# Graph network of four layers on one core: a 256-column scratch fill behind every gather, and fetch places as 16-bit floats

## The reference

```
h = relu(layernorm(x));  x += clip(h + segment_sum(h[src] * edge_weight * w, dst) + 0.1 * h, 0, 1)
h = relu(layernorm(x));  x += h + silu(bilinear(h, segment_sum(silu(bilinear(h[dst], edge_attr_8)) @ W, src))) @ W'
h = relu(layernorm(x));  x += segment_sum((h[src] @ W_rel[edge_type]) * e, dst)       # 90 relations
h = relu(layernorm(x));  w = MLP(edge_attr_6) -> (E, 16, 16)
for i in range(4):       h = gelu(mean over dst of (h[src] @ w) + h @ root_W[i] + root_b[i])
x += h
```

## Time and profile before

| what | value |
|---|---|
| median of 3 runs | 28610.86 us (28602.41 to 28721.83) |
| the profiled execution's own time | 28730.07 us |
| its span, first to last instruction | 28728.3 us |
| PE matmul busy | 22502.9 us (78%) |
| POOL busy | 21497.8 us (75%) |
| DVE busy | 17590.5 us (61%) |
| ACT busy | 14192.2 us (49%) |
| mean granted TensorE clock | 0.864 of full speed |
| HBM traffic | 109 GB/s over the span |

### The profile page before, as it was taken

The page is one execution under the profiler, slowest core; times in us unless marked ns, Lnnn a source line. Parts: engine busy times, 40 slices in busy tenths (PEclk is TensorE's granted clock), DMA queues, the critical chain, the costliest instruction groups (busy, mean ns, idle before and its releaser), DMA issues. The chain is left out here.

```text
span 28728.3 us, 413713 instructions
## 1 busy us (share of the span) xinstructions
PE 22502.9 (78%) x109882; PEld 12362.4 (43%) x109882; DVE 17590.5 (61%) x29340; ACT 14192.2 (49%) x24676; POOL 21497.8 (75%) x31473
## 2 busy tenths in 40 slices
PE   7888668888878888867777777688886888778886
PEld 3444345555545555533434344333333333333333
DVE  5555468888867667744444444566665666656665
ACT  6666511111135444533333333477775777667775
POOL 7888878888867667766667677677777777777777
PEclk9999879999988888877778787799898889888898
DMA  3211235555532222222222222455554555555554
GB/s 98 45 45 44 46 74 92 94 92 94 92 68 66 64 64 65 66 62 87 90 88 94 87 91 92 125 173 173 174 172 142 172 172 174 158 156 171 172 172 138
DMA packets 2201230, 3120.14 MB, mean 109 GB/s; under 512 B 782486, under 2 KB 1548644, under 8 KB 2199460
## 3 DMA queue, kind: packets, MB, share of 16 engines
q1 hardware_dynamic: 1340898, 2927.73, 31.3%
q0 software_dynamic: 790944, 162.36, 8.3%
q10 hardware_dynamic: 69282, 28.92, 0.4%
HBM read 2443.85 MB, written 673.47 MB: 109 GB/s over the span
## 5 line engine op out<-in xcount | busy, mean ns | idle before, releaser
L772 POOL DMA_INDIRECT got<-table,idx x14310 | 14075.9, 984 | 6055.7 <-issue 3081.4
L790 PE MATMUL in_place<-place_hot,tparts 128*128 128x512 fp8e4 (+1 forms) x49950 | 12106.4, 399 | 2647.8 <-ACT place_hot L995 1563.8
L995 ACT ACTIVATE place_hot<-place_b,far_lanes 128x512 fp8e4<-128x512 f32 (+1 forms) x17550 | 10586.2, 683 | 8.8 <-PE in_place L790 8.8
L790 PEld LDWEIGHTS in_place<-place_hot,tparts 128*128 128x128 bf16 x49950 | 5100.3, 105 | 9003.7 <-issue 4843.7
L1599 POOL DMA_INDIRECT added<-rows,add_idx x2160 | 3602.4, 1668 | 714.3 <-issue 654.5
L968 ACT ACTIVATE mask<-contw 128x208 f32 (+2 forms) x1350 | 555.9, 412 | 5970.6 <-DVE run L1129 2705.2
L775 POOL MEMSET rest<- 128x128 f32 (+2 forms) x14310 | 3199.8, 224 | 10.2
L1216 DVE TENSOR_TENSOR prod<-wcopy,got 128x1024 f32<-128x1024 f32 x810 | 991.5, 1227 | 2990.9 <-ACT wcopy L947 1895.6
L1642 PE MATMUL acc<-hot,spread 128*128 128x392 bf16 x12960 | 2545.4, 350 | 0.0
L1107 DVE SCALAR_TENSOR_TENSOR picked<-range_b,range_col,in_place 128x512 f32<-128x512 f16 (+1 forms) x1350 | 962.7, 713 | 2553.8 <-DMA added<-rows,add_idx 2404.6
L1171 DVE TENSOR_TENSOR prod<-w_in,rows_p 128x2048 f32<-128x2048 f32 x810 | 1846.8, 2280 | 444.7 <-ACT rows_p L983 283.7
(11 more groups left out here) (250 smaller groups left out, 21896.4 us busy)
## 6 DMA issues: line engine op xcount, KB each, us to landing
w_in<-kept SPq DMA_DIRECT2D x2430, 512.0 KB
kept<-wcopy SPq DMA_DIRECT2D x810, 512.0 KB
place_b<-place_row SPq DMA_DIRECT2D x1080, 256.0 KB
got<-table,idx POOLq DMA_INDIRECT x14310
attr<-in_edge_attr SPq DMA_DIRECT2D x270, 768.0 KB
range_b<-range_row SPq DMA_DIRECT2D x1080, 128.0 KB
rows<-in_src_row SPq DMA_DIRECT2D x270, 512.0 KB
sums<-outb SPq DMA_DIRECT2D x1350, 96.0 KB
```

The lines of the kernel that those rows point to most:

```text
L772: pool.indirect_dma_start(out=got[:, r, j * W:(j + 1) * W], out_offset=None, in_=table, in_offset=bass.IndirectOffsetOnAxis(ap=idx[:, r, j ...
L790: mm = pe.matmul(in_place[b][:, h, :], tparts[:, s, t, :], place_hot[:, b, t, h * XC:(h + 1) * XC], start=(t == 0 and s == 0), stop=(t == ...
L995: ins = act.activation(place_hot[:, b, t, :], place_b[:, b, :], ACT.Abs_reciprocal_sqrt, bias=SB["far_lanes"][:, t:t + 1], scale=HOT_SLOPE ...
```

## The change

All gathering passes get a fill of 256 columns. The weighted pass has that width already; relational and kernel_kept had 128, kernel_net 32. The row of places is stored and loaded as 16-bit floats. The shift of 2^-12, which a 16-bit place of up to 1,567 could not carry, moves into the bias column `far_lanes`, so that the same argument comes out. Places are whole numbers below 2,048 and stand exactly in 16 bits. No instruction is added, taken away or moved on any engine: one DVE instruction of the preparation (an addition over 3,240 columns) becomes a copy with a cast.

```
+RW = 256
...
-        place_row = dram("place_row", (EP + 2 * CE,))
+        place_row = dram("place_row", (EP + 2 * CE,), F16)
...
-        range16 = sb("range16", [P, T], F16)
+        range16, place16 = sb("range16", [P, T], F16), sb("place16", [P, T], F16)
...
-                for row, v in ((SB["place_row"], key), (SB["range_row"], range16)):
+                for row, v in ((SB["place_row"], place16), (SB["range_row"], range16)):
...
-                c.step(dve.tensor_scalar(key[:, :], key[:, :], PLACE_SHIFT, None, ALU.add))
+                c.step(dve.tensor_copy(place16[:, :], key[:, :]))
...
-        rest = sb("rest", [P, {"weighted": 256, "relational": 128, "kernel_net": 32, "kernel_kept": 128}[kind] * J0])
+        rest = sb("rest", [P, J0 * RW])
         src_at = sb("src_at", [P, T], I32)
-        RW = rest.shape[1] // J0
...
-            place_b = sb("place_b", [P, HALVES, XE])
+            place_b = sb("place_b", [P, HALVES, XE], F16)
...
-        "const_far_lanes": -lanes() * np.float32(HOT_SLOPE),
+        "const_far_lanes": (PLACE_SHIFT - lanes()) * np.float32(HOT_SLOPE),
```

## The result

The changed kernel takes 27848.6 us (median of 4 runs, 27823.51 to 27856.5) where the kernel before takes 28660.6 beside it: a ratio of 0.9715 [0.9688, 0.9742]. It is 2.8% **faster**. The profiled execution took 27823.5 us, with a span of 27821.7.

A forecast was written before the change was run, and what follows sets the result against it. POOL bounds the weighted pass, the ACT, PE and DVE ring the kept ones; elsewhere POOL's idle time covers wider fills. Terms 0 + 0 + 20 + 90 = +110 us on 28611 gave 28720 us, 0.4% longer; forecast 28640 to 28800, range 28560 to 28950.

The forecast's parts named there:

- What bounds the kernel now: All passes: POOL limits the weighted pass; elsewhere it waits for indices, 310 to 1011 us a pass, cover for wider fills.
- Covered three times over: 0: Relational pass: wider fills add 260 us of POOL, hidden by 816 us of its idle time, so 0.
- single waits of 29 us: kernel_net: POOL's single index waits reach 29 us, read as users going very unevenly, so the ring can run dry.
- I take 20, close to the low end: kernel_net: fills add 635 us of POOL against 930 us of cover; +20 us from a range of 0 to 635.
- I take 90, near the middle: Three kept passes: 253 us more POOL each overruns the cover; +90 us, between 62 and 132 in all.
- The floor: Kept passes: POOL's wider fills overrun its cover by 28, 16 and 18 us, so POOL becomes the limit by a hair.
- two stages so nearly equal ... give a bit more than the longer: Kept passes: POOL and the ACT, PE, DVE ring, nearly equal, take slightly more than the longer; supports +90 us.
- Places, 0: Place loads: halving them to 16 bits gains 0, as loads land early; upper bound 540 us in the relational pass.
- The ring was not cooled: Kept passes, rival: starved ring idles PE, cold starts cost 1.7 us each; 230 us, 28950 in all; chance 0.22.
- DVE was not held up: Kept passes, rival: fills lengthen DVE copies by 0.117 us each; up to 190 us, 28910 in all; chance 0.08.
- The 0.10 for "faster": Relational pass, rival: halved place loads save 1 us a chunk, 270 us, giving 28450 us; chance 0.10.
- The last sentence: Signs of error: relational under 4000 us or kept under 3329 means place loads or gather pace mattered in an unseen way.

The follow-up runs named there:

- e1: Kernel before with fills of 256 columns in all passes, places still 32-bit; 27812 us, 0.9659 of the kernel before.
- e3: Kernel before with the 256-column fill in the relational pass alone, places 32-bit; 28261 us, 0.9812 of the kernel before.
- e10: The changed kernel, unchanged, on a chip where the kernel before takes 29286 us; 27800 us, 0.9485 of the kernel before.
- e17: Kernel before plus one wide POOL fill at each chunk's end (relational 1100 columns, kernel_net 2600), where before takes 29402 us; 28110 us, 0.9563.
- e2: Kernel before with the change's 16-bit places and the old fill widths; 28732 us, 0.9990 of the kernel before.
- e5: Kernel before plus useless DVE reductions in each relational and kernel_net chunk, where before takes 26311 us; 27119 us, 1.0306.
- e6: Kernel before plus one wide POOL fill at each chunk's end (relational 1100 columns, kernel_net 2600), where before takes 26311 us; 27140 us, 1.0314.
- e13: Kernel before plus one wide POOL fill at each relational and kernel_net chunk's end, where before takes 26303 us; 27139 us, 1.0319.
- e8: Fills of 128 columns in weighted, 160 in relational and kept, 64 in kernel_net, where the kernel before takes 26311 us; 26444 us, 1.0050.

## Why the prediction was wrong, point by point

**"What bounds the kernel now"** was read rightly in this: outside the weighted pass POOL waited for indices. What was wrong is the silent step behind it, that idle time is cover and nothing else. Two rows were misread beside it, without weight in the sum. The 94 us wait of the weighted pass lies ahead of the first gather and so outside the 3375 us, which gathers, fills and 546 us of issue fill without it. The 143.6 us wait of the relational pass lies ahead of its first gather too, so the cover there was 816 - 143 = 673 us, still 2.6 times the 260. What ends the 7.24 us for which ACT idles in the kept ring was left open; it is a late signal of PE.

**Relational pass, "Covered three times over: 0".** This is the step that failed. The term was 0 and measured -441 us. The cost of the fills was right, 339 ns and +260 us; the ring beside it was taken as fixed at 15.6 us a chunk. It was not: of two kinds of chunk, 13 and 20 us, the slower was full of PE's pauses. When POOL was made last at 13.95 us, the 20-us chunks went, and with them all the pauses, or most of them on chips C and E. The even pace is shorter than the uneven mean. e1, e3, e10 and e17 show that it is POOL's work in this pass that does it; e2 that it is not the places; e17 that it is not the distance.

**kernel_net, "I take 20, close to the low end".** Measured -347 us. Again the fills were right. The prediction took single waits of 29 us for a sign that the users go very unevenly. The 29.1 us were one wait ahead of the first gather, and it is there after as well (29.3); within the pass the longest was 18.7 us. The unevenness itself was real, but it was no risk of running dry; it was time that the ring lost. The mechanism there is less clear than in the relational pass. Beyond the 1352 gaps of the program some 80 pauses are left before, far too few for 347 us, and the clock did not rise. The 470 late signals (1831 us) are gone after, but e17 still has 440 and the shortest kernel_net of a slow chip. That the swing went is shown (4.5 us to 0.25), what drove it is open.

**Kept passes, "I take 90, near the middle".** Measured -20 in the sum of three. The floor was worked out well: POOL did become last (waits for indices 310 to 1.1 us, `rows_p` 12.7 in all three passes to 857.8 in the first alone), and each pass sits at 12.3 us a chunk. The fault was in "two stages so nearly equal ... give a bit more than the longer": they gave just POOL's time, and the pauses and late signals, which had stood in the ring's own 12.3 us, went. On chips B and D the same pass runs at 11.48 us without them, so there the wide fill costs 223 us a pass (3098 to 3321), near the 253 of the prediction.

**Places, 0**: right (e2, 0.9990). By the Trainium skill (ScalarE: Activation LUTs, What ACT_TABLE_LOAD costs) an ACTIVATE takes one element per cycle and lane, for fp32 and bf16 alike; the trace shows that fp16 costs no more than fp32 either, 683 ns for both.

**The rivals.** The ring was not cooled: the kept clock is 0.90 before and after. DVE was not held up: 2268.5 us of work in the first kept pass before, 2272.0 after. Its rows had been misread: the DVE instruction of 0.67 us ran beside a gather (1511.88 to 1512.83), and of the 520 such instructions (L1090) of 0.6 us and more in the weighted pass before, all started during a gather and none during a fill, beside which they take 0.17 us on the mean. The 0.10 for "faster" was given to the place loads, which did nothing; that the time came out faster does not bear that rival out. The last sentence named a relational pass under 4000 us as the sign of something not seen, "the pace of the gathers" among it; that came true, but had no chance of its own. It should have had one.

**What is shown and what is open.** Shown: the kernel before takes 26.3 to 29.4 ms, depending on the chip, and the changed kernel the same wherever it ran, C, D and the chip of the case (27.80 to 27.85 ms; the fills alone 27.81 on A), since POOL sets its pace. Shown: on the slow chips PE pauses in the relational and kept passes of the kernel before, on the fast ones none of eight kernels has more than one pause in a fetching pass, and none has a late signal. Not shown: what the pauses and the late signals are, and which of them costs the time. The pauses come within long runs of matmuls, without a semaphore, and all or most of them go when POOL is last by its own work; something outside PE that the core must share would fit, and so would a supply of instructions that can't keep up. Nor is it excluded that the recording of the trace has a part: for the semaphore that is `w_made` in two of the passes, the trace before has 2504 raises where 2727 recorded matmuls make one, and each trace of a slow chip lacks some (2275 to 2514 are there), while those of the fast chips have them all (2731 to 2741, other uses with them). No run tells these apart. Also not shown is the kernel before itself in a profile of a fast chip; only its time and the kept passes of e5, e6 and e13 stand for it. There its relational pass can be estimated from e8, where POOL waits for indices only once (143 us) and the 160-column fill takes 253 ns: at the 232 ns of 128 columns, 2429 fills are 51 us less than 3578, near 3530 us. If so, the prediction's sum without any cover, +260, +635 and three times +253 us (1654), is near what the change costs on such a chip, 1501 us.

No version tried beats both kernels on every chip. The changed kernel (or e1) is the best where the kernel before takes over 28 ms, the kernel before where it takes 26.3.

## What to carry to other kernels

Idle time of an engine is cover only if the rest of the loop has a pace of its own that doesn't depend on it. Look at the spread of the chunk times before the mean: chunks of 13 and 20 us in a loop whose work is the same each time say that something is being lost that no busy time shows, and a filler on the engine that is ahead can buy it back. But such a filler gives a floor to every chip: here it is worth 2.8% where the case was timed and some 5% on chip C (e10), and costs 5.7% on chip D, so measure on more than one before keeping it. And where a profile names a releaser that can't be, look up which semaphore the wait is for, and who raises it when.

## What the runs showed of the hardware that was not expected

- The same program takes 26303 us on one chip and 29402 on another, 11.8% apart, the runs of one chip within some 0.5% of each other. When one engine's own instructions set the pace, the chips agree within 0.2% (27800 to 27849).
- TensorE (PE) stops between matmuls that wait for nothing the trace shows, for 0.24 to 0.69 us each in the stretch above, on some chips only, up to 955 times in one pass.
- On the same chips a semaphore that PE raises can come late. In the kernel before, one came 5.40 us after the recorded end of its matmul, and 265 waits in the first kept pass (1604 us) end with one over 1 us late. Eight kernels on the two fast chips have no such wait.
- An engine with more to do can take such stops away: on chip C 64 columns more per fill turned a weighted pass of 3579 us into one of 3367.
